# Batch 0's preparation in a fused cross-attention layer: all context loaded at once, key splits on VectorE, group 0's stack filled alone, twelve maxima inside quarter 0

## The chip, the cores and the metric

One core of a Trainium2 chip runs the whole program. The engines are TensorE (PE in the rows; PEld is its weight load), VectorE (DVE), ScalarE (ACT), GpSimd (POOL) and SyncE (SP), which in this kernel only issues DMAs. The metric is the device time of one execution in microseconds, lower is better.

## What is computed

Sixteen batches of a transformer layer with cross-attention: 512 queries and 1601 context rows of width 256, 16 heads of 16, and an MLP of width 1024, all in float32.

```python
B, Lq, _ = Q.shape
Lkv = KV.shape[1]
qn = _layer_norm(Q, ln_q_g, ln_q_b)
q = (qn @ Wq + bq).reshape(B, Lq, H, DH).transpose(0, 2, 1, 3)
k = (KV @ Wk + bk).reshape(B, Lkv, H, DH).transpose(0, 2, 1, 3)
v = (KV @ Wv + bv).reshape(B, Lkv, H, DH).transpose(0, 2, 1, 3)
scores = jnp.einsum('bhqd,bhkd->bhqk', q, k) / jnp.sqrt(jnp.float32(DH))
attn = jax.nn.softmax(scores, axis=-1)
ctx = jnp.einsum('bhqk,bhkd->bhqd', attn, v)
ctx = ctx.transpose(0, 2, 1, 3).reshape(B, Lq, D)
x = Q + (ctx @ Wo + bo)
h = _layer_norm(x, ln_ff_g, ln_ff_b)
ff = jax.nn.silu(h @ W1 + b1) @ W2 + b2
x = x + ff
```

## The kernel before

**Heads.** A batch has four quarters, one for each group of four heads (q = 0 to 3). Eight heads are a half (s = q // 2), with their own `k_stack[s]`, `q_stack[s]` and `v_sb[s]`. The context is handled in chunks c = 0 to 3 of 512, 512, 512 and 65 keys, and in 13 tiles of 128 keys; a quarter has 26 units, two for each tile.

**Scores in bf16.** Each key and query is split into three bf16 parts (`k_parts`, `q_parts`). ScalarE writes the float32 value to one of two buffers `whole` and the first part (L662, L663). GpSimd makes the other two with three subtractions (`read_parts`, L513 to L516) and counts them in `split`; ScalarE waits for the split before the last one, since `whole` has two buffers. SP then copies the parts by DMA into six 16-row slots of the stacks: `place` issues 12 DMAs for the first three slots of a group (L389), and `repeat`, which waits until all 24 of a group's `place` DMAs landed, issues six that copy the slots that repeat a part (L401).

**Maxima.** The softmax is shifted by the row's maximum. TensorE makes the scores once in the other orientation, 52 pieces m for a group (`make_rows`, L995, into two buffers `rows_ps`); VectorE reduces each (`read_rows`, L830). When 52 are in, VectorE negates them, TensorE turns them ("turn", L944), ScalarE copies them to `shift_parts`, and SP places them as three more rows of `q_stack` (`place_shift`, L424). The scores proper (L1010) wait for that. In steady state the maxima of the next group are made inside a quarter, 40 in units up to 19 and the first 12 (`EARLY`) of the group after it in the rest; `plan` spreads four over each tile.

**Side steps.** Everything else goes through the one PSUM bank `side`, in a fixed order of steps: TensorE fills it, ScalarE (for some steps VectorE) reads it, and TensorE waits (`side_read`) for the step before. Context transposes (`ctx`), keys (`k`), values (`v`), transposes of the normalised x (`x`) and queries (`q`) are steps.

**The opening of batch 0** is the `prologue` of each engine, and all is in program order on each. SP issues wk, context chunks 0 and 1, x, the other weights, seven columns of biases and gains (L366), two rows and eight small pieces; only then chunks 2 and 3, which reuse the buffers `ctx_nat` of the first two; then the stacks of both groups of half 0 (`fill_stacks`). TensorE makes the eight context steps, waits for all 22 loads (`loaded`), makes the product for the output bias (L1047), keys 0 to 3, x, the query and the four value steps; then 26 maxima of group 0, 26 more with the keys and the query of half 1 among them, the turn, and 12 maxima of group 1. VectorE sets the rows of ones in both stacks (L851), waits for all loads, and takes the moments of x. GpSimd normalises x and then splits the keys. Quarter 0 follows.

## Time and profile before

| | us |
|---|---|
| median of three runs | 3767.32 |
| lowest, highest | 3766.78, 3767.60 |
| profiled execution, its own time | 3763.43 |
| its span in the profile | 3761.6 |
| mean granted clock of TensorE | 0.989 |

The span is what the trace covers. In a row of the timeline, the first number is the start in us, the second the busy time, `x4` the number of instructions merged, and the bracket the idle time before them on that engine and what ended it. A float32 matmul shows as several records.

### The profile page before, as it was taken

The numbers are of one execution on the slowest core, as the hardware profiler recorded it, in microseconds if no ns is written. First come the engines' busy times: TensorE is split into PE (matmuls) and PEld (weight loads), VectorE is DVE, ScalarE is ACT, GpSimd is POOL, SyncE is SP. The second block draws the span as 40 slices with busy tenths as digits, with TensorE's granted clock in tenths as the row PEclk, the third lists the DMA queues.
The fourth block names the chain that finished last, engine by engine and source line by source line (L and its number), as shares of the span: only waits on it lengthen the run. The fifth ranks groups of instructions, "written<-read, shape, count | busy, mean of one in ns | idle before, by whom it ended". The sixth has DMA issues, their size and how long they took to land.

```text
span 3761.6 us, 52959 instructions
## 1 busy us (share of the span) xinstructions
PE 3559.0 (95%) x19880; PEld 1605.0 (43%) x19880; DVE 2483.2 (66%) x4568; ACT 2242.9 (60%) x2979; POOL 901.5 (24%) x1323
## 2 busy tenths in 40 slices
PE   3899999999999999999999999999999999999996
PEld 2233444444434444444444434444444444444434
DVE  2777767666676766667666676766667676676751
ACT  1366666656666565666656666566656656666562
POOL 2122313212231222313122231212313112231101
PEclk8899999999999999999999999999999999999999
DMA  3222212222122321212222122322212232121200
GB/s 84 45 50 40 46 32 61 41 47 45 32 51 39 65 41 32 47 33 58 41 58 38 30 50 37 64 41 36 49 32 54 42 64 39 27 48 34 41 7 12
DMA packets 121409, 162.99 MB, mean 43 GB/s; under 512 B 36912, under 2 KB 102464, under 8 KB 118080
## 3 DMA queue, kind: packets, MB, share of 16 engines
q1 hardware_dynamic: 121152, 159.60, 21.7%
q8 instruction: 157, 2.57, 0.3%
q14 instruction: 100, 0.82, 0.1%
HBM read 46.43 MB, written 8.39 MB: 15 GB/s over the span
## 4 chain that ended last, share of the span: by engine, by line
PE 81%; DVE 11%; ACT 4%; issue 2%; SPq 1%; POOL 1%; DMA 0%; ACTq 0%; POOLq 0%; DVEq 0%
PE o_ps L1029 20%; PE rows_ps L995 19%; PE scores L1010 14%; DVE chunk_max L830 8%; PE side L972 6%; PE side L969 6%; PE side L958 5%; PE side L950 4%; PE side L962 3%; ACT probs L717 2%; PE side L954 2%; DVE stats L748 1%; DVE resid L775 1%; PE side L941 1%; ACT ctxT L633 1%
## 5 line engine op out<-in xcount | busy, mean ns | idle before, releaser
L830 DVE TENSOR_REDUCE chunk_max<-rows_ps 128x1 f32<-128x512 f32 (+1 forms) x3328 | 2124.4, 666 | 1132.9 <-PE rows_ps L995 1124.4
L717 ACT ACTIVATE probs<-scores 128x1024 f32<-128x1024 f32 (+1 forms) x1664 | 1676.0, 1023 | 1174.5 <-PE scores L1010 1167.1
L995 PE MATMUL rows_ps<-k_stack,q_stack 96*128 96x512 bf16 (+1 forms) x4096 | 1220.1, 339 | 94.1 <-DVE chunk_max L830 50.6
L1010 PE MATMUL scores<-q_stack,k_stack 99*128 99x512 bf16 (+1 forms) x3328 | 1033.6, 379 | 3.3 <-ACT probs L717 2.7
L1029 PE MATMUL o_ps<-probs,v_sb 128*32 128x512 f32 x6656 | 886.5, 605 | 0.4 <-ACT probs L717 0.4
L995 PEld LDWEIGHTS rows_ps<-k_stack,q_stack 96*128 96x128 bf16 x4096 | 334.3, 97 | 1164.2 <-DVE chunk_max L830 930.7
L1010 PEld LDWEIGHTS scores<-q_stack,k_stack 99*128 99x128 bf16 (+1 forms) x3328 | 325.0, 100 | 300.4 <-issue 38.2
L513 POOL TENSOR_TENSOR rest<-whole,k_parts 128x512 f32<-128x512 f32 (+1 forms) x128 | 120.6, 942 | 1002.4 <-ACT k_parts L663 997.2
L565 POOL TENSOR_TENSOR attT<-o_sb,denom 128x512 f32<-128x512 f32 x64 | 81.2, 1268 | 945.3 <-DVE denom L817 945.3
L969 PE MATMUL side<-hT,w_sb 128*128 128x256 f32 x1024 | 272.6, 380 | 11.8 <-ACT tanh_sb L675 9.9
L972 PE MATMUL side<-w_sb,ffT 128*128 128x256 f32 x1024 | 259.2, 381 | 5.6 <-DVE ffT L793 5.0
L1029 PEld LDWEIGHTS o_ps<-probs,v_sb 128*32 128x32 f32 x6656 | 131.0, 108 | 296.8 <-issue 222.2
L958 PE MATMUL side<-wv_sb,ctxT 128*128 128x128 f32 (+1 forms) x1664 | 242.3, 278 | 4.6 <-ACT v_sb L649 2.0
L958 PEld LDWEIGHTS side<-wv_sb,ctxT 128*128 128x128 f32 (+1 forms) x1664 | 226.0, 187 | 46.7 <-ACT v_sb L649 11.4
L950 PE MATMUL side<-ctxT,wk_sb 128*128 128x512 f32 (+1 forms) x512 | 222.7, 519 | 9.2 <-ACT k_parts L663 9.2
L969 PEld LDWEIGHTS side<-hT,w_sb 128*128 128x128 f32 x1024 | 192.9, 190 | 63.2 <-ACT tanh_sb L675 17.0
L972 PEld LDWEIGHTS side<-w_sb,ffT 128*128 128x128 f32 x1024 | 191.5, 189 | 56.5 <-issue 7.7
L673 ACT ACTIVATE ffT<-side,half_b 128x256 f32<-128x256 f32 x256 | 121.5, 475 | 111.5 <-PE side L969 108.8
L528 POOL TENSOR_TENSOR newton<-rstd 128x2 f32<-128x2 f32 (+1 forms) x144 | 28.1, 195 | 591.6 <-DVE half_var L763 584.0
L962 PE MATMUL side<-wo_pad,attT 128*128 128x256 f32 x512 | 139.7, 389 | 5.0 <-POOL attT L565 3.9
L675 ACT ACTIVATE tanh_sb<-side,half_b 128x256 f32<-128x256 f32 x256 | 121.7, 475 | 0.0
L514 POOL TENSOR_TENSOR k_parts<-whole,k_parts 128x512 bf16<-128x512 f32 (+1 forms) x128 | 121.1, 946 | 0.1
(68 smaller groups left out, 1971.3 us busy)
## 6 DMA issues: line engine op xcount, KB each, us to landing
k_stack<-k_parts SPq DMA_DIRECT2D x768, 50.0 KB, 2.2
k_stack<-k_stack SPq DMA_DIRECT2D x192, 200.1 KB, 5.6
ctx_nat<-in_ctx SPq DMA_DIRECT2D x48, 512.0 KB, 4.0
q_stack<-q_parts SPq DMA_DIRECT2D x768, 16.0 KB, 1.8
q_stack<-q_stack SPq DMA_DIRECT2D x192, 64.0 KB, 3.4
x_nat<-in_x SPq DMA_DIRECT2D x16, 512.0 KB, 6.1
resid<-in_x SPq DMA_DIRECT2D x32, 256.0 KB, 2.8
out<-resid SPq DMA_DIRECT2D x32, 256.0 KB, 2.5
```

The costliest lines, as they stand in the source:

```text
L673: nc.scalar.activation(ffT[:, m, :], side[:, cols], ACT.Identity, bias=half_b1[:, m:m + 1], scale=0.5)
L675: last = nc.scalar.activation(tanh_sb[:, cols], side[:, cols], ACT.Tanh, bias=half_b1[:, m:m + 1], scale=0.5)
L717: nc.scalar.activation(probs[0:rows, (q + t) % 2, 2 * LQ * pair:2 * LQ * (pair + 1)], scores[0:rows, 2 * LQ * pair:2 * LQ * (pair + 1)], A ...
L830: nc.vector.tensor_reduce(dst, src, AX.X, ALU.max).then_inc(rows_read, 1)
L950: ins = nc.tensor.matmul(side[:, 0:width(arg)], wk_sb[:, j, P * s:P * (s + 1)], ctxT[:, j, CHUNK * arg:CHUNK * arg + width(arg)], start=(j ...
L958: ins = nc.tensor.matmul(side[0:rows, P * t:P * (t + 1)], ctxT[:, j, P * i:P * i + rows], wv_sb[:, j, P * s:P * (s + 1)], start=(j == 0), ...
L962: ins = nc.tensor.matmul(side[:, D * i:D * (i + 1)], attT[:, j, q0:q0 + P], wo_pad[:, j, :], start=(j == 0), stop=(j == 3))
L969: ins = nc.tensor.matmul(side[:, QH * i:QH * (i + 1)], w1_sb[:, j, P * m:P * (m + 1)], hT[:, j, :], start=(j == 0), stop=(j == KC - 1))
L972: ins = nc.tensor.matmul(side[:, D * i:D * (i + 1)], ffT[:, j, P * i:P * (i + 1)], w2_sb[:, j, :], start=(j == 0), stop=(j == FM - 1))
L995: last = nc.tensor.matmul(rows_ps[:, m % 2, d0:d0 + w], q_stack[s][0:STACK, h, P * t:P * (t + 1)], k_stack[s][0:STACK, h, k0:k0 + w], star ...
L1010: ins = nc.tensor.matmul(scores[0:keys_in(t), LQ * j:LQ * (j + 1)], k_stack[s][:, h, P * t:P * t + keys_in(t)], q_stack[s][:, h, :], start ...
L1029: last = nc.tensor.matmul(o_ps[32 * j:32 * j + 32, :], v_sb[q // 2][0:rows, t, col:col + 32], probs[0:rows, (q + t) % 2, LQ * j:LQ * (j + 1)],
```

## The change

- SP issues context chunk 0 first, then wk, chunk 1, x, chunks 2 and 3, wq and four columns; `loaded_first` counts wk, wq and the four columns (6). wv, the rows, the small pieces, w1, w2 and three columns follow and are counted in `loaded` (16). Chunks 2 and 3 go into a part of `ffT`, unused at that time, with semaphores of their own (`ctx_beside`).
- The steps follow a list `PROLOGUE`: context, k0, k1, v0, k2, v1, k3, v2, x0, x1, q0, v3, then half 1's keys and query among the maxima. TensorE and ScalarE wait for `loaded_first` before k0; TensorE waits for `loaded` before v0.
- VectorE takes the moments of x first, sets one stack's rows, splits half 0's four key chunks (`split_keys`), sets the other stack's rows. GpSimd keeps the query's split and half 1's.
- SP places group 0's keys, then repeats group 0; ScalarE issues group 0's 12 `place` DMAs of queries after the query's split. Group 1 follows on SP. `place` takes the queue as an argument and is defined once for both engines.
- The 12 maxima of group 1 move from the prologue into the first six tiles of quarter 0, six in a tile there instead of four.
- The product for the output bias moves behind the values, ahead of the maxima.

Lines of context are left out; declarations of the new semaphores and the removed local copy of `place` too.

```diff
@@ -57,7 +57,8 @@
-N_LOADS = 5 + 7 + 2 + 8
+N_FIRST = 2 + 4
+N_LOADS = 3 + 3 + 2 + 8
@@ -102,7 +103,13 @@
-BEFORE = sum(len(PREPARE[q]) for q in (1, 2, 3)) + 1
+PROLOGUE = ([(0, "ctx", (c, kc)) for c in range(NCH) for kc in range(KC)] + [(0, "k", 0), (0, "k", 1)]
+            + [(0, "v", 0), (0, "k", 2), (0, "v", 1), (0, "k", 3), (0, "v", 2), (0, "x", 0), (0, "x", 1), (0, "q", 0), (0, "v", 3)]
+            + [(1, "k", c) for c in range(NCH)] + [(1, "q", 0)])
+BESIDE_MAXIMA = NCH + 1
+BEFORE = len(PROLOGUE) + 1
@@ -157,6 +164,10 @@
+AHEAD = 2
@@ -170,11 +181,12 @@
-def plan(steps):
-    units, slot = [], 0
+def plan(steps, opening=False):
+    units, slot = [], -EARLY if opening else 0
+        per_tile = PER_TILE + AHEAD * (opening and t < EARLY // AHEAD)
@@ -185,7 +197,7 @@
-            while placed < PER_TILE and done * PER_TILE >= (placed + MAX_PHASE) * sum(costs):
+            while placed < per_tile and done * per_tile >= (placed + MAX_PHASE) * sum(costs):
@@ -357,16 +372,32 @@
+        def place(queue, dst, src, rows, g):
+            for part in range(PARTS):
+                slot = rows.index(part)
+                for h in range(4 * (g % 2), 4 * (g % 2) + 4):
+                    queue.dma_start(dst[16 * slot:16 * slot + 16, h, :], src[16 * h:16 * h + 16, part, :])\
+                        .then_inc(placed[g], 16)
-            def column(dst, src, n):
+            def column(dst, src, n, landed):
-                    sp.dma_start(dst[:, 0:n], src.rearrange("(c p) -> p c", p=P)).then_inc(loaded, 16)
+                    sp.dma_start(dst[:, 0:n], src.rearrange("(c p) -> p c", p=P)).then_inc(landed, 16)
-                if c < NCH - 1:
+                if b == 0 and c >= 2:
+                    dst = ffT[:, 4 * (c - 2):4 * (c - 2) + 4, :]
+                    if c < NCH - 1:
+                        sp.dma_start(dst, ctx[b, CHUNK * c:CHUNK * (c + 1), :].rearrange("(t p) d -> p t d", p=P))\
+                            .then_inc(ctx_beside[c - 2], 16)
+                    else:
+                        sp.dma_start(dst[0:LAST, 0, :], ctx[b, CHUNK * c:LK, :]).then_inc(ctx_beside[c - 2], 16)
+                elif c < NCH - 1:
@@ -406,13 +429,13 @@
-                place(k_stack[s], k_parts, K_ROWS, 2 * s)
+                place(sp, k_stack[s], k_parts, K_ROWS, 2 * s)
-                place(q_stack[s], q_parts, Q_ROWS, 2 * s)
-                place(k_stack[s], k_parts, K_ROWS, 2 * s + 1)
+                place(sp, q_stack[s], q_parts, Q_ROWS, 2 * s)
+                place(sp, k_stack[s], k_parts, K_ROWS, 2 * s + 1)
-                place(q_stack[s], q_parts, Q_ROWS, 2 * s + 1)
+                place(sp, q_stack[s], q_parts, Q_ROWS, 2 * s + 1)
@@ -432,15 +455,16 @@
-                sp.dma_start(wk_sb[:, :, :], wk.rearrange("(c p) n -> p c n", p=P)).then_inc(loaded, 16)
+                sp.dma_start(wk_sb[:, :, :], wk.rearrange("(c p) n -> p c n", p=P)).then_inc(loaded_first, 16)
-                for dst, src in ((wq_sb, wq), (wv_sb, wv), (w1_sb, w1), (w2_sb, w2)):
-                    sp.dma_start(dst[:, :, :], src.rearrange("(c p) n -> p c n", p=P)).then_inc(loaded, 16)
-                for dst, src, n in ((bq_c, bq, KC), (bk_c, bk, KC), (b1_c, b1, FM), (gq_c, gq, KC), (cq_c, cq, KC),
-                                    (gf_c, gf, KC), (cf_c, cf, KC)):
-                    column(dst, src, n)
+                load_ctx(0, 2)
+                load_ctx(0, 3)
+                sp.dma_start(wq_sb[:, :, :], wq.rearrange("(c p) n -> p c n", p=P)).then_inc(loaded_first, 16)
+                for dst, src, n in ((bk_c, bk, KC), (bq_c, bq, KC), (gq_c, gq, KC), (cq_c, cq, KC)):
+                    column(dst, src, n, loaded_first)
+                sp.dma_start(wv_sb[:, :, :], wv.rearrange("(c p) n -> p c n", p=P)).then_inc(loaded, 16)
@@ -451,11 +475,18 @@
-                for c in (2, 3):
-                    sp.wait_ge(side_ready, index(PREPARE[1], "ctx", (c - 2, KC - 1)) + 1)
-                    load_ctx(0, c)
-                fill_stacks(0, 0)
+                for dst, src in ((w1_sb, w1), (w2_sb, w2)):
+                    sp.dma_start(dst[:, :, :], src.rearrange("(c p) n -> p c n", p=P)).then_inc(loaded, 16)
+                for dst, src, n in ((b1_c, b1, FM), (gf_c, gf, KC), (cf_c, cf, KC)):
+                    column(dst, src, n, loaded)
+                sp.wait_ge(split, NCH)
+                place(sp, k_stack[0], k_parts, K_ROWS, 0)
+                repeat(0, 0)
+                place(sp, k_stack[0], k_parts, K_ROWS, 1)
+                place(sp, q_stack[0], q_parts, Q_ROWS, 1)
+                repeat(0, 1)
@@ -578,17 +609,15 @@
-                for s in range(2):
-                    pool.memset(v_sb[s][:, :, :], 1.0).then_inc(ones_set, 1)
+                pool.memset(v_sb[0][:, :, :], 1.0).then_inc(ones_set, 1)
+                normalise_x(0)
+                pool.memset(v_sb[1][:, :, :], 1.0).then_inc(ones_set, 1)
+                for n, (s, kind, arg) in enumerate(PROLOGUE):
+                    if (s, kind) == (0, "q") or s == 1:
+                        read_parts(0, s, (0, 0), n, arg if kind == "k" else NCH)
-                normalise_x(0)
-                n = 0
-                for q, (_, s) in ((1, PREPARED[1]), (2, PREPARED[2]), (3, PREPARED[3])):
-                    splits(0, s, (0, n), PREPARE[q])
-                    n += len(PREPARE[q])
@@ -684,18 +713,25 @@
-                n = 0
-                for q in (1, 2, 3):
-                    for k, (_, _, kind, arg) in enumerate(PREPARE[q]):
-                        if (q, kind, arg) == (1, "k", 0):
-                            act.wait_ge(loaded, 16 * N_LOADS)
-                            nc.scalar.mul(bq_c[:, :], bq_c[:, :], 1.0 / DH ** 0.5).then_inc(setup_done, 1)
-                            nc.scalar.mul(half_b1[:, :], b1_c[:, :], 0.5).then_inc(setup_done, 1)
-                            act.wait_ge(setup_done, 3)
-                            act.wait_ge(ones_set, 4)
-                        side_step(0, PREPARED[q][1], (0, n), k, kind, arg)
-                    n += len(PREPARE[q])
+                for n, (s, kind, arg) in enumerate(PROLOGUE):
+                    if (s, kind, arg) == (0, "k", 0):
+                        act.wait_ge(loaded_first, 16 * N_FIRST)
+                        nc.scalar.mul(bq_c[:, :], bq_c[:, :], 1.0 / DH ** 0.5).then_inc(setup_done, 1)
+                        act.wait_ge(setup_done, 1)
+                    if (s, kind, arg) == (0, "v", 0):
+                        act.wait_ge(ones_set, 1)
+                    if (s, kind, arg) == (1, "k", 0):
+                        act.wait_ge(loaded, 16 * N_LOADS)
+                        nc.scalar.mul(half_b1[:, :], b1_c[:, :], 0.5).then_inc(setup_done, 1)
+                        act.wait_ge(setup_done, 2)
+                    side_step(0, s, (0, 0), n, kind, arg)
+                    if (s, kind) == (0, "q"):
+                        act.wait_ge(split, NCH + 1)
+                        place(act, q_stack[0], q_parts, Q_ROWS, 0)
+                n = len(PROLOGUE)
@@ -801,6 +837,19 @@
+            def split_keys(c):
+                w, off = width(c), CHUNK * c
+                src, parts = whole[:, c % 2, 0:w], [k_parts[:, part, off:off + w] for part in range(PARTS)]
+                dve.wait_ge(side_read, PROLOGUE.index((0, "k", c)) + 1)
+                wait(dve, split, c)
+                seq.inc(nc.vector.tensor_tensor(rest[:, 0:w], src, parts[0], ALU.subtract))
+                seq.inc(nc.vector.tensor_tensor(parts[1], src, parts[0], ALU.subtract))
+                dve.wait_ge(dve_seq, seq.value)
+                nc.vector.tensor_tensor(parts[2], rest[:, 0:w], parts[1], ALU.subtract).then_inc(split, 1)
@@ -844,32 +893,33 @@
+                for stage in range(STAGES):
+                    x_moments(0, stage)
+                for s in range(2):
+                    nc.vector.memset(k_stack[s][STACK:ROWS, :, :], 1.0).then_inc(stack_ones, 1)
+                    if s == 0:
+                        for c in range(NCH):
+                            split_keys(c)
-                nc.vector.memset(ones, 1.0).then_inc(setup_done, 1)
-                for s in range(2):
-                    nc.vector.memset(k_stack[s][STACK:ROWS, :, :], 1.0).then_inc(ones_set, 1)
+                nc.vector.memset(ones, 1.0).then_inc(bv_spread, 1)
-                dve.wait_ge(setup_done, 3)
+                dve.wait_ge(bv_spread, 1)
-                for stage in range(STAGES):
-                    x_moments(0, stage)
-                for m in range(EARLY):
-                    read_rows(0, 1, m)
-                for u, work in enumerate(plan(steps)):
+                for u, work in enumerate(plan(steps, b == q == 0)):
@@ -919,7 +969,10 @@
-                        pe.wait_ge(ctx_landed[arg[0] % 2], b * 32 + 16 * (arg[0] // 2 + 1))
+                        if b == 0 and arg[0] >= 2:
+                            pe.wait_ge(ctx_beside[arg[0] - 2], 16)
+                        else:
+                            pe.wait_ge(ctx_landed[arg[0] % 2], 16 if b == 0 else b * 32 - 16 + 16 * (arg[0] // 2 + 1))
@@ -938,7 +991,8 @@
-                    ins = nc.tensor.transpose(side[:, P * t:P * t + rows], ctx_nat[0:rows, c % 2, t, P * j:P * (j + 1)],
+                    place_of = ffT[:, 4 * (c - 2):4 * (c - 2) + 4, :] if b == 0 and c >= 2 else ctx_nat[:, c % 2, :, :]
+                    ins = nc.tensor.transpose(side[:, P * t:P * t + rows], place_of[0:rows, t, P * j:P * (j + 1)],
@@ -1034,36 +1088,39 @@
-                n, m = 0, 0
-                for q in (1, 2, 3):
-                    for k, (_, _, kind, arg) in enumerate(PREPARE[q]):
-                        if (q, kind, arg) == (1, "k", 0):
-                            pe.wait_ge(ones_set, 4)
-                            pe.wait_ge(loaded, 16 * N_LOADS)
-                            pe.wait_ge(bv_spread, 4)
-                            for g in range(4):
-                                last = nc.tensor.matmul(o_ps[:, 0:D], probs[:, 0, P * g:P * (g + 1)], wo_pad[:, g, :],
-                                                        start=(g == 0), stop=(g == 3))
-                            last.then_inc(bo_product, 1)
-                        if q == 3:
-                            while m < FIRST_MAXIMA + 5 * k:
-                                make_rows(0, 0, m)
-                                m += 1
-                        side_step(0, PREPARED[q][1], (0, n), k, kind, arg)
-                    n += len(PREPARE[q])
+                m, beside = 0, len(PROLOGUE) - BESIDE_MAXIMA
+                for n, (s, kind, arg) in enumerate(PROLOGUE):
+                    if (s, kind, arg) == (0, "k", 0):
+                        pe.wait_ge(loaded_first, 16 * N_FIRST)
+                    if (s, kind, arg) == (0, "v", 0):
+                        pe.wait_ge(loaded, 16 * N_LOADS)
+                    if n == beside:
+                        pe.wait_ge(bv_spread, 5)
+                        for g in range(4):
+                            last = nc.tensor.matmul(o_ps[:, 0:D], probs[:, 0, P * g:P * (g + 1)], wo_pad[:, g, :],
+                                                    start=(g == 0), stop=(g == 3))
+                        last.then_inc(bo_product, 1)
+                    if n >= beside:
+                        while m < FIRST_MAXIMA + 5 * (n - beside):
+                            make_rows(0, 0, m)
+                            m += 1
+                    side_step(0, s, (0, 0), n, kind, arg)
-                for m in range(EARLY):
-                    make_rows(0, 1, m)
+                pe.wait_ge(stack_ones, 2)
+                pe.wait_ge(ones_set, 2)
-                for u, work in enumerate(plan(steps)):
+                for u, work in enumerate(plan(steps, b == q == 0)):
```

On VectorE, at the start of the program, before: ones, both stacks' rows of ones, `bv` spread, the output bias, moments of x.

```order
L848 MEMSET denom 128x128
L851 MEMSET k_stack 3x12808 x2
L856 TENSOR_SCALAR probs<-denom,bv_pad 128x128 x4
L860 TENSOR_TENSOR bo_row<-o_ps,bo_row 128x256
L748 BN_STATS stats<-x_nat 128x6 x4
L756 BN_AGGR moments<-stats 128x2 x4
```

On VectorE, at the start of the program, now:

```order
L784 BN_STATS stats<-x_nat 128x6 x4
L792 BN_AGGR moments<-stats 128x2 x4
L795 TENSOR_SCALAR half_var<-moments 128x4
L797 TENSOR_SCALAR rstd<-half_var 128x4
L799 TENSOR_SCALAR half_var<-half_var 128x4
L900 MEMSET k_stack 3x12808
L848 TENSOR_TENSOR rest<-whole,k_parts 128x512
L849 TENSOR_TENSOR k_parts<-whole,k_parts 128x512
L851 TENSOR_TENSOR k_parts<-rest,k_parts 128x512
```

The moments moved ahead of everything, one stack's ones stand between them and the splits, and three subtractions for each chunk are new there; the other stack's ones come behind the last split.

On SP, behind the loads, the filling of half 0's stacks before (groups 0 and 1: keys, queries, repeats) and the shift of group 0:

```order
L389 DMA k_stack<-k_parts 16x1601 x12
L389 DMA q_stack<-q_parts 16x512 x12
L389 DMA k_stack<-k_parts 16x1601 x12
L401 DMA k_stack<-k_stack 16x6404 x3
L401 DMA q_stack<-q_stack 16x2048 x3
L389 DMA q_stack<-q_parts 16x512 x12
L401 DMA k_stack<-k_stack 16x6404 x3
L401 DMA q_stack<-q_stack 16x2048 x3
L424 DMA q_stack<-shift_parts 1x4x512 x3
```

On SP, the same place now:

```order
L380 DMA k_stack<-k_parts 16x1601 x12
L424 DMA k_stack<-k_stack 16x6404 x3
L424 DMA q_stack<-q_stack 16x2048 x3
L380 DMA k_stack<-k_parts 16x1601 x12
L380 DMA q_stack<-q_parts 16x512 x12
L424 DMA k_stack<-k_stack 16x6404 x3
L424 DMA q_stack<-q_stack 16x2048 x3
L447 DMA q_stack<-shift_parts 1x4x512 x3
```

Group 0's repeats stand behind its 12 key DMAs alone; its 12 query DMAs left this queue for ScalarE's, and all of group 1 comes after.

On TensorE, from the last maxima of group 0 into quarter 0, before:

```order
L944 MATMUL side<-ident_bf,neg_parts 12x128 x4
L995 MATMUL rows_ps<-k_stack,q_stack 128x512 x12
L1010 MATMUL scores<-q_stack,k_stack 128x512 x2
L995 MATMUL rows_ps<-k_stack,q_stack 128x65 x4
L958 MATMUL side<-wv_sb,ctxT 128x128 x4
```

On TensorE, the same place now:

```order
L998 MATMUL side<-ident_bf,neg_parts 12x128 x4
L1064 MATMUL scores<-q_stack,k_stack 128x512 x2
L1049 MATMUL rows_ps<-k_stack,q_stack 128x512
L1012 MATMUL side<-wv_sb,ctxT 128x128 x2
L1049 MATMUL rows_ps<-k_stack,q_stack 128x512
L1012 MATMUL side<-wv_sb,ctxT 128x128 x2
```

The maxima between the turn and the first scores are gone from there, and one stands between every two products of the values.

## Rows read from the trace of the kernel before

**Rows 1.** The page, its chain that ended last, by engine:
```profile
PE 81%; DVE 11%; ACT 4%; issue 2%; SPq 1%; POOL 1%; DMA 0%; ACTq 0%; POOLq 0%; DVEq 0%
```
**Rows 2.** The chain in order of time, 0 to 150 us: start, us, what:
```profile
42.92 4.84 POOL x_nat L533 x4
...
89.10 2.69 DMA q_stack<-q_stack
...
91.92 0.60 PE rows_ps L995
...
109.62 3.57 PE side L950 x4
...
136.97 0.58 PE side L944 x4
```
**Rows 3.** Busy time by windows (PE, PEld, DVE, ACT, POOL; granted clock, DMA share, GB/s):
```profile
92.00:113.00 21.00, 18.21 (x37) 4.07 (x37) 16.16 (x26) 0.00 (x0) 0.00 (x0) 0.50 0.31 47
```
**Rows 4.** The timeline, 0 to 31 us: context steps and SP's issues:
```profile
5.74 1.09 PE L941 MATMUL side<-ident,ctx_nat 128*128 128x128 f32 x4 [5.74 <-DMA ctx_nat<-in_ctx]
...
9.30 1.12 PE L941 MATMUL side<-ident,ctx_nat 128*128 128x128 f32 x4 [0.68 <-ACT ctxT L633]
...
12.04 3.60 SPq L366 DMA_DIRECT2D gq_c<-in_L_xattn_ln_q_g  x1
...
22.16 0.43 SPq L371 DMA_DIRECT2D ctx_nat<-in_ctx  x1
...
30.73 0.37 PE L941 MATMUL side<-ident,ctx_nat 65*128 65x65 f32 x1 [0.30 <-ACT ctxT L633]
```
**Rows 5.** DMA issues, 0 to 35 and 59 to 92 us: KB each, us to landing:
```profile
x_nat<-in_x SPq DMA_DIRECT2D x1, 512.0 KB, 7.6
...
q_stack<-q_parts SPq DMA_DIRECT2D x16, 16.0 KB, 1.8
```
**Rows 6.** The timeline, 44 to 67 us: steps of keys, x, query, values:
```profile
44.19 1.98 PE L950 MATMUL side<-ctxT,wk_sb 128*128 128x512 f32 x4 [1.35 <-ACT k_parts L663]
...
57.40 1.12 PE L948 MATMUL side<-ident,x_nat 128*128 128x128 f32 x4 [0.87 <-ACT qnT L637]
...
59.38 3.63 PE L954 MATMUL side<-qnT,wq_sb 128*128 128x512 f32 x4 [0.87 <-ACT qnT L637]
...
67.09 2.05 PE L958 MATMUL side<-wv_sb,ctxT 128*128 128x128 f32 x16 [0.68 <-ACT v_sb L649]
```
**Rows 7.** The timeline of SP's queue, 59 to 92 us:
```profile
67.92 7.84 SPq L389 DMA_DIRECT2D q_stack<-q_parts  x12
...
83.39 2.52 SPq L401 DMA_DIRECT2D k_stack<-k_stack  x3
```
**Rows 8.** VectorE: its timeline, 0 to 40 us, and a group by line:
```profile
3.70 10.73 DVE L851 MEMSET k_stack<- 3x12808 bf16 x1 [2.72 <-issue]
17.05 10.73 DVE L851 MEMSET k_stack<- 3x12808 bf16 x1 [2.62 <-issue]
...
36.82 1.39 DVE L748 BATCH_NORM_STATS2 stats<-x_nat 128x6 f32<-128x256 f32 x4
...
39.07 0.17 DVE L763 TENSOR_SCALAR half_var<-half_var 128x4 f32<-128x4 f32 x1
...
L793 DVE SCALAR_TENSOR_TENSOR ffT<-tanh_sb,ffT 128x512 f32<-128x512 f32 x128 | 87.5, 683 | 47.4 <-ACT tanh_sb L675 47.4
```
**Rows 9.** The timeline, 137 to 146 us: the shift's issues, the first scores:
```profile
138.19 1.90 SPq L424 DMA_DIRECT2D q_stack<-shift_parts  x3
...
145.46 1.06 PE L1010 MATMUL scores<-q_stack,k_stack 99*128 99x512 bf16 x2
```
**Rows 10.** The timeline of quarter 0, 161 to 166 us:
```profile
161.94 0.61 PE L995 MATMUL rows_ps<-k_stack,q_stack 96*128 96x512 bf16 x2
...
163.11 0.39 PE L995 MATMUL rows_ps<-k_stack,q_stack 96*128 96x512 bf16 x1 [0.35 <-DVE chunk_max L830]
...
165.73 2.52 DVE L830 TENSOR_REDUCE chunk_max<-rows_ps 128x1 f32<-128x512 f32 x4 [0.84 <-PE rows_ps L995]
```

9 lines of the change are left out of this document (3 added, 6 removed).

## The prediction, made before the changed kernel was run

> **What bounds the kernel now.** I read the page first: the profiled execution has a span of 3761.6 us (the table), and TensorE (PE) carries most of the chain that ended last [rows 1]. So a change outside the steady quarters can only shorten the opening. I then read the chain of waits for the first 150 us. It shows three things to look for. GpSimd's four normalisations stand on it (42.92 us), then DMA issues up to 89.10 us, and only at 91.92 us does TensorE compute the first row of scores for the maxima [rows 2]. The 21 us behind run at a granted clock of 0.50, the 1.2 GHz level, with TensorE and VectorE taking turns [rows 3]. Everything before 91.92 us is latency on a chain of single steps. That chain is what the change rebuilds; nothing in it touches batches 1 to 15.
>
> The sum goes by stages: the first row (91.92 us before), the stretch from there to the turn (45.05 us, from 91.92 to 136.97), the turn up to the first scores, and quarter 0.
>
> **Loading and transposing.** Before, chunks 2 and 3 of the context were issued behind 21 other loads, at 22.16 us [rows 4], and TensorE stood still for them. Now all four chunks are near the head of SP's queue. The first chunk's transposes began at 5.74 us [rows 4]; it is now issued half a microsecond earlier and ahead of wk's 256 KB, for which I take 4.9 us (bounds 4.4 and 5.7). In a row of the timeline, the busy time and the idle time before it together are the repeat time of a step: 1.12 + 0.68 = 1.80 us for four transposes and their copy, 0.37 + 0.30 = 0.67 for 65 columns [rows 4]. Six and two of them: 10.8 + 1.3, so the keys can begin at 17.0 us. They need six early loads, two weights and four columns of biases and gains. Before, the column loads were held in SP's queue (gq's issue took 3.60 us [rows 4]) behind 4.25 MB; now 2.6 MB stand ahead of them. x took 7.6 us to land with 1.3 MB ahead of it [rows 5], so 2.6 MB should be in by 12 us. I take no wait; the bound is 1.2 us, for a landing at 18.2, a little behind the end of gq's issue before, 15.6.
>
> **Keys, values and queries, now interleaved on the one bank `side`.** TensorE and ScalarE alternate, so each step costs its repeat time. A step of keys: 1.98 + 1.35, 3.34 us with rounding. The same four matmuls take 1.99 us at 2.4 GHz and 3.63 us at 1.2 GHz (the query step), so the first, after transposes at the low level, costs 4.98. A step of values: 2.05 + 0.68 = 2.73 us. The two x steps: 1.12 + 0.87 = 1.99 us each at the low level [rows 6]. The 65-column key step lies between 0.67 and 3.34; I take 1.2, because its matmuls are an eighth as long. On the path: k0 4.98, k1 3.34, v0 2.73, k2 3.34, v1 2.73, k3 1.2, v2 2.73 = 21.05, which brings 38.0 us; x0 and x1 (3.98) make it 42.0. From the first query matmul to SP's first issue of query parts it was 59.38 to 67.92 = 8.54 us [rows 6, 7] (matmuls, two activations, GpSimd's three subtractions; the query's split stays on GpSimd, and there is nothing ahead of it there). That gives 50.6 us at the low level throughout; with the high level kept after the keys it is 2.6 us less (1.0 on x, 1.65 on q). Context transposes with a gap of 0.7 us never left the low level, keys with gaps of 1.4 us kept the high one. I take the middle, 49.2 us.
>
> What hides beside this path? First, VectorE's split of the keys, taken from GpSimd. Moments of x start when x lands, at 9.9 us, and take 2.4 (36.82 to 39.24 [rows 8]); then comes the memset of k_stack's last three rows. The profile gives that memset as 10.73 us, but the two of them start at 3.70 and 17.05, 13.35 us apart, and the gap of 2.62 us between is put down to nothing [rows 8]. I take 13.35, so VectorE is free at 25.7 us and splits chunk 0 by 27.8 (three operations of 0.68 us, the nearest row being the product of two SBUF operands [rows 8]). ScalarE needs that split before it writes k2's result, at 30.0 us. Slack 2.2 us. The other splits keep up, the last ends about 36.2 us, and SP issues group 0's keys from then to 43.8, before the queries are ready. By the Trainium skill (VectorE: DVE Perf Modes, Zero memsets can be issued as uint32) a memset takes one cycle per element whatever the type, 12808 of them at 0.96 GHz, an estimate of 13.3 us; this trace agrees by the distance of the starts, not by the row's own length. By the row alone VectorE would be free at 23.1 and the slack 4.8, with the same total.
>
> Second, TensorE's wait before v0 for all 16 remaining loads, at 25.3 us. Behind it stand v0, k2 and all that follows. The 2 MB of w1 and w2, formerly early, are now issued after the small loads. Before, the queue was through with the same loads at 22.16 us [rows 4], and 4 us more let them land. With less stall in the columns, of which gq's alone held 3 us, I put it at 24, so no cost; bounds 0 and +6. Third, normalised x: moments at 12.3 plus 8.5 us on GpSimd (39.24 to 47.76 [rows 2, 8]), 20.8, needed at 38. Fourth, ScalarE's and TensorE's product for the output bias: VectorE's second memset now starts at 36.2 and ends at 49.6; its inputs follow in 1 us and TensorE's eight matmuls take 3.8, so 55, before the rows.
>
> **Filling group 0.** Before, SP issued q parts (7.84 us), then group 1's keys (twelve more), then the repeated slots. Now ScalarE issues the q parts at 49.2 and SP goes straight to the repeats, which wait for them. At SP's 0.65 us an issue that is 7.84 [rows 7]; the last is issued at 56.5 and lands 1.8 us later [rows 5]: 58.3. From SP's first repeat to TensorE's first row it was 83.39 to 91.92 = 8.53 us [rows 2, 7]. First row: **66.8 us, 25.1 earlier**. No issue by ScalarE is in this trace. Its price is bounded by the cheapest and the dearest issue of SP: 0.43 and 3.60 us [rows 4]; I take 0.65, the same transfers. The Trainium skill (DMA: Bandwidth & Descriptors, Issuing engines are not separate DMA queues) says that a second issuing engine saves only the sequencer's time. Here SP is idle from 43.8 us, so by that this part saves nothing; what saves 7.8 us is that group 1's keys no longer stand ahead of the repeats.
>
> Behind the repeats SP issues group 1's parts (from 64.6, 7.84 each: keys to 72, queries to 80, landed by 82). ScalarE's first key of the second half overwrites them and waits for that; it comes at 66.8 + 17.7 + 3.6 = 88.1 (before, 91.92 to 109.62, and 3.57 of matmuls [rows 2]). Slack 6 us, and nothing else in it changed. So the 45.05 us stretch should be the same.
>
> **Turn and quarter 0.** Before, 12 maxima of group 1 ran from 137.55 to the first scores at 145.46 [rows 9] and hid the shift's way. Now scores follow the turn directly and wait for it: the three issues began at 138.19 and took 1.90, and the last of them, begun at 139.5, needs 1.8 to land and 0.1 to wake TensorE: 141.4 in the old time [rows 5, 9]. Gain 4.1 us. The 12 maxima go into tiles 0 to 5 of quarter 0, two more in each. In tiles 0 to 2, TensorE is busy throughout with values: one matmul of a row takes 0.39, two 0.61 [rows 10], so one more costs 0.22 and a tile 0.45. Tiles 3 to 5 repeat every 3.36 us or little more, with four reads of 2.52 us and 0.84 idle on VectorE [rows 10]; six reads take 3.78 and some 0.4 idle remains: +0.9 a tile. Sum 4.0, plus 0.4 for a start at 1.2 GHz after an idle TensorE: **+4.4**. Bounds: 12 x 0.22 = 2.6, and 12 x 3.36 / 4 = 10.1, where each costs a quarter of a tile.
>
> **Sum.** -25.1 - 4.1 + 4.4 = -24.8 us. The profiled execution took 3763.43 us (span 3761.6), the median of the three runs is 3767.32; by the span I expect 3736.8, by the median **3742.5**.
>
> **Rivals.**
> 1. *The loads set v0.* If the last of the 16 lands at 31 us, the path is 5.7 us later: 3748. For it: a column's issue took 3.60 us, and b1's 1024 small elements are now among the last. Against it: less data ahead. In the range.
> 2. *The maxima cost nothing in quarter 0 and issues are cheap.* Lower bounds, -1.8 for quarter 0, -2.6 for ScalarE's issues (0.43 each), -1.3 for the clock: 3737.
> 3. *The gain is given back behind the first row.* If group 1's filling is 20 us later than I put it, the first key of the second half waits 14 us and the total is about 3757; with 24 us it is 3761, no change. Nothing in the rows is that slow.
> 4. *Slower.* One mechanism: ScalarE's queue pays for each of its twelve issues what gq's column cost, 3.60 us. Then q is in place 35.4 us later, and the total is 3742.5 + 35.4 = 3778. It decides from 0.65 + 24.8 / 12 = 2.7 us an issue. Against it: that price was paid with 4 MB queued, and here the rings are empty.
> 5. *The change does not do what it says,* as VectorE's splits or v0 wait for something unseen for over 17 us: near 3760.
>
> **How the numbers follow.** Forecast 0.70, rival 1 0.13, rival 2 0.09, rivals 3 and 5 0.05, rival 4 0.03. The range takes in the forecast's bounds and rivals 1 and 2: 3733 to 3753. A difference within 0.2%, 7.5 us, is about what a measurement of this kernel can't tell from none. Faster 0.93, same 0.04, slower 0.03.
>
> **What would show it.** In the changed kernel's trace: context transposes from 5 to 17 us without a pause; v0's matmuls at about 25 us; SP's first key parts at 36, ScalarE's issues at 49, the first row at 67; the first scores about 50 us after it, some 4 us behind the turn; quarter 0 some 4.4 us longer; from there on the same rows 24.8 us earlier. What would make me wrong: an issue on ScalarE that costs far from 0.65 us, v0 held by the loads, or tiles 0 to 5 that grow by over 1 us each.

## The result, and the profile after

The changed kernel takes 3745.86 us (median of 4 runs, 3743.92 to 3747.18), the kernel before, run beside it, 3767.46 (4 runs, 3766.78 to 3768.86). The ratio is 0.9942 [0.9925, 0.9959]: 21.6 us faster. The forecast was 3742.5, with 3733 to 3753 as its range.

The profiled execution of after took 3746.01 us, with a span of 3744.2, 17.4 less than before. Its page, the chain that ended last by engine; GpSimd and SP's queue, with 1% each before [rows 1], stand at 0%:

```profile
PE 82%; DVE 11%; ACT 4%; issue 2%; DMA 0%; POOL 0%; SPq 0%; ACTq 0%; DVEq 0%
```

The chain in order of time, 0 to 120 us (start, us, what), answers to [rows 2]:

```profile
0.72 4.06 DMA ctx_nat<-in_ctx
4.92 1.10 PE side L995 x4
...
17.09 3.77 PE side L1004 x4
...
22.26 3.79 PE side L1004 x4
...
37.59 2.06 PE side L1012 x16
...
43.37 3.69 PE side L1008 x4
...
58.98 1.83 DMA q_stack<-q_parts
...
66.45 2.64 DMA q_stack<-q_stack
...
117.16 1.78 DMA q_stack<-shift_parts
119.07 1.01 PE scores L1064 x2
```

The four normalisations on GpSimd that stood at 42.92 us are gone from it. From 4.92 us on the path is the one bank `side`, TensorE and ScalarE in turn, as the forecast had it. The queue rows on SP and ScalarE (timeline, 38 to 118 us) answer to [rows 7, 9]:

```profile
38.22 8.21 SPq L380 DMA_DIRECT2D k_stack<-k_parts  x12
...
51.96 7.63 ACTq L380 DMA_DIRECT2D q_stack<-q_parts  x12
...
60.83 2.40 SPq L424 DMA_DIRECT2D k_stack<-k_stack  x3
...
69.23 1.01 PE L1049 MATMUL rows_ps<-k_stack,q_stack 96*128 96x512 bf16 x2 [12.51 <-DMA q_stack<-q_stack]
...
115.45 2.30 SPq L447 DMA_DIRECT2D q_stack<-shift_parts  x3
...
119.07 1.01 PE L1064 MATMUL scores<-q_stack,k_stack 99*128 99x512 bf16 x2 [4.26 <-DMA q_stack<-shift_parts]
```

Laid beside the same marks of before, in us from the span's start:

| mark | before | after | difference |
|---|---|---|---|
| chunk 2's first transposes | 26.50 | 12.06 | -14.4 |
| first key matmuls | 36.23 | 17.09 | -19.1 |
| query matmuls | 59.38 | 43.37 | -16.0 |
| first issue of the queries' parts | 67.92 | 51.96 | -16.0 |
| SP's repeats begin | 83.39 | 60.83 | -22.6 |
| first row | 91.92 | 69.23 | -22.7 |
| turn | 136.97 | 114.23 | -22.7 |
| first scores | 145.46 | 119.07 | -26.4 |
| shift at the end of quarter 0 | 188.57 | 168.31 | -20.3 |
| shift of the last quarter but one | 3642.70 | 3623.26 | -19.4 |
| end of the span | 3761.6 | 3744.2 | -17.4 |

So the opening and quarter 0 gave 20.3 us. The other 2.9 us of this pair lie where the change touches nothing: about 0.9 in the steady quarters, mostly one wait of TensorE for a context load (0.51 us before, at 1523; 1.53 us after, at 1504), and 2.0 in the last 119 us. There the granted clock differs, as the windows of the last 10 us show (busy time of PE, PEld, DVE, ACT, POOL; clock; DMA share; GB/s), before and then after:

```profile
3751.60:3761.60 10.00, 6.65 (x31) 5.51 (x29) 0.69 (x1) 0.00 (x0) 0.00 (x0) 1.00 0.08 26
```
```profile
3734.20:3744.20 10.00, 6.61 (x25) 5.26 (x23) 0.69 (x1) 0.00 (x0) 0.00 (x0) 0.84 0.08 26
```

Over the profiles below, this end (shift of the last quarter but one to the end of the span) took 118.9 to 124.4 us. It adds to any comparison of single executions, so the experiments are read by their marks before it.

### The profile page after: what moved, and what is told of

Same layout as the page of the kernel before. It is cut to its first block, busy times and chain, and to the rows that moved or that the text cites. A ratio compares the mean times of both kernels' runs of the same rounds, so it can differ in the third digit from the quotient of the medians.

```text
span 3744.2 us, 52962 instructions
## 1 busy us (share of the span) xinstructions
PE 3560.6 (95%) x19880; PEld 1608.2 (43%) x19880; DVE 2488.8 (66%) x4580; ACT 2243.0 (60%) x2979; POOL 890.5 (24%) x1311
## 4 chain that ended last, share of the span: by engine, by line
PE 82%; DVE 11%; ACT 4%; issue 2%; DMA 0%; POOL 0%; SPq 0%; ACTq 0%; DVEq 0%
PE o_ps L1083 20%; PE rows_ps L1049 19%; PE scores L1064 14%; DVE chunk_max L879 8%; PE side L1026 6%; PE side L1023 6%; PE side L1012 5%; PE side L1004 5%; PE side L1016 3%; ACT probs L753 2%; PE side L1008 2%; DVE stats L784 1%; DVE resid L811 1%; PE side L995 1%; ACT ctxT L662 1%
## 5 line engine op out<-in xcount | busy, mean ns | idle before, releaser
L544 POOL TENSOR_TENSOR rest<-whole,k_parts 128x512 f32<-128x512 f32 x124 | 116.8, 942 | 995.0 <-ACT k_parts L692 990.5
L829 DVE SCALAR_TENSOR_TENSOR ffT<-tanh_sb,ffT 128x512 f32<-128x512 f32 x128 | 87.5, 683 | 47.4 <-ACT tanh_sb L704 47.4
```

## The experiments

Nine kernels make one edit each, all on the changed kernel but one; two try a faster order; one is the changed kernel again. What is read from each, in us ("to turn" runs from the first row to the turn, "scores to shift" from the first scores to SP's issue of the shift at the end of quarter 0, and "shift at" is the time of that issue):

| kernel | first row | to turn | turn to scores | scores to shift | shift at |
|---|---|---|---|---|---|
| before | 91.92 | 45.05 | 8.49 | 43.11 | 188.57 |
| changed | 69.23 | 45.00 | 4.84 | 49.24 | 168.31 |
| changed again (e12) | 68.73 | 45.16 | 4.76 | 49.04 | 167.69 |
| e1 maxima back | 69.50 | 45.16 | 8.49 | 44.61 | 167.76 |
| e2 splits on GpSimd | 67.19 | 45.16 | 4.84 | 49.00 | 166.19 |
| e3 queries by SP | 67.13 | 45.16 | 4.36 | 47.63 | 164.28 |
| e4 context late | 80.18 | 45.14 | 4.76 | 49.00 | 179.08 |
| e5 group 1's keys first | 67.61 | 44.72 | 4.84 | 48.89 | 166.06 |
| e6 busy turn | 67.12 | 43.54 | 4.83 | 46.97 | 162.46 |
| e7 busy opening | 69.12 | 44.86 | 4.77 | 47.75 | 166.50 |
| e8 busy before rows | 67.29 | 44.93 | 4.76 | 49.14 | 166.12 |
| e9 maxima alone, on before | 90.73 | 43.52 | 4.26 | 48.90 | 187.41 |
| e10 queries first | 60.13 | 46.63 | 4.36 | 49.20 | 160.32 |
| e11 both | 59.87 | 45.15 | 4.76 | 47.38 | 157.16 |

**How far an opening repeats itself.** The changed kernel, e12, e1 and e6 have the same instructions up to the first row, which came at 69.23, 68.73, 69.50 and 67.12. The difference stands in one row of the timeline, the second chunk's key matmuls. First the changed kernel's:

```profile
22.26 3.78 PE L1004 MATMUL side<-ctxT,wk_sb 128*128 128x512 f32 x4 [1.42 <-ACT k_parts L692]
```

and e6's:

```profile
22.26 1.98 PE L1004 MATMUL side<-ctxT,wk_sb 128*128 128x512 f32 x4 [1.42 <-ACT k_parts L692]
```

They start in the same hundredth, with the same matmuls and waits before them, and took 3.78 us at the 1.2 GHz level and 1.98 at 2.4. The changed kernel, e12 and e1 drew the first, e2 to e6 and e8 the second. What sets it isn't visible in the rows. e12's own pair of readings doesn't decide between chance and its rival, since both executions of the changed kernel drew the low level; that e6, and up to this step e3, e5 and e8 too, drew the high one with the same instructions speaks for chance. Openings are therefore compared with others that drew the same: 67.1 to 67.6, or 68.7 to 69.5.

Of each edit only the telling lines are shown. ` ...` marks lines left out; the definitions of the extra matmuls and, in e1, the matching lines of VectorE are left out too.

**e4: chunks 2 and 3 of the context loaded behind the other loads, as before.**

```
-                load_ctx(0, 2)
-                load_ctx(0, 3)
 ...                                     (wq, wv, the columns, wo, bv)
+                load_ctx(0, 2)
+                load_ctx(0, 3)
```

> The changed kernel with context chunks 2 and 3 issued last of all loads (at some 19.3 us, behind the column whose issue took 3.78 us). My theory: the chain from loads to queries is what sets the first row, so it moves by what the transposes of chunk 2 move: from 12.06 to 23.5 us, 11.5 us later, less 1 to 2 us because TensorE may be quicker after it; the first row at 80. Rival: another chain (VectorE's memset and splits, SP's key parts) is as long, and the first row moves by less than 6 us.

Its timeline, 10 to 26 us:

```profile
10.25 1.12 PE L995 MATMUL side<-ident,ctx_nat 128*128 128x128 f32 x4 [0.68 <-ACT ctxT L662]
25.29 1.09 PE L995 MATMUL side<-ident,ffT 128*128 128x128 f32 x4 [13.93 <-DMA ffT<-in_ctx]
```

TensorE stands 13.93 us for the load. Chunk 2 begins 13.2 us later than in the changed kernel (12.06), and the first row comes at 80.18, 13.1 behind e6's like-clocked 67.12: the delay passes through whole. Of the first row's 22.7 us, the context's early load carries 13.

**e5: group 1's keys placed before the repeats again.**

```
-                repeat(0, 0)
                 place(sp, k_stack[0], k_parts, K_ROWS, 1)
+                repeat(0, 0)
```

> The changed kernel with group 1's key parts on SP ahead of group 0's repeats, as before the change. In the changed kernel SP idles from 46.4 us until the queries have landed at 60.8. My theory: the 7.5 us of issues fit into that idle time, and the first row stays at 69.2 us; what the prediction gave to filling group 0 alone was really won by the queue being empty that early. Rival, the prediction's words: group 1's keys ahead of the repeats cost 7.5 us, first row at 76.7.

The two queues, 36 to 62 us:

```profile
36.47 16.02 SPq L380 DMA_DIRECT2D k_stack<-k_parts  x24
...
50.31 7.64 ACTq L380 DMA_DIRECT2D q_stack<-q_parts  x12
...
59.19 2.40 SPq L424 DMA_DIRECT2D k_stack<-k_stack  x3
```

All 24 issues fit between the keys' readiness at 36.5 and 52.5, while the queries are still being issued; the repeats wait for those at 59.19. The first row is at 67.61, 0.4 to 0.5 behind the others. The query matmuls alone took 3.78 here and 3.36 in e6, which covers that. As long as the queries are issued by another engine, filling group 0 alone is worth nothing.

**e3: group 0's queries issued by SP**, between group 0's keys and the repeats, and group 1 behind them.

```
+                sp.wait_ge(split, NCH + 1)
+                place(sp, q_stack[0], q_parts, Q_ROWS, 0)
 ...
-                        act.wait_ge(split, NCH + 1)
-                        place(act, q_stack[0], q_parts, Q_ROWS, 0)
```

> The changed kernel with group 0's twelve query placements issued by SP, behind its key parts, instead of by ScalarE. SP is idle from 46.4 to 60.8 us there. My theory: the same first row, 69.2 us within 0.3, since the issues begin at 52.0 either way. Rival: ScalarE's queue is what lets them start early; then the first row is 1 us or more later.

```profile
36.56 8.50 SPq L380 DMA_DIRECT2D k_stack<-k_parts  x12
...
50.01 7.46 SPq L380 DMA_DIRECT2D q_stack<-q_parts  x12
...
58.71 2.40 SPq L424 DMA_DIRECT2D k_stack<-k_stack  x3
```

First row 67.13, the same. SP is idle from 45.1 to 50.0, so it is no help that ScalarE takes these twelve issues. e3 and e5 each remove one of two measures and lose nothing. Before, the twelve issues of group 1's keys stood between the queries and the repeats, where they cost the 6.6 us by which that way shortened (67.92 to 83.39, now 51.96 to 60.83). Either measure moves them from there. With both undone they would stand on the path again; that was not tried.

**e2: key splits back on GpSimd.**

```
-                    if (s, kind) == (0, "q") or s == 1:
+                    if kind in ("k", "q"):
 ...
-                    if s == 0:
-                        for c in range(NCH):
-                            split_keys(c)
```

> The changed kernel with half 0's key splits back on GpSimd (3.5 us a chunk instead of 2.1). My theory: with values between the keys the splits have slack on either engine. GpSimd is free at 21.5 us, splits chunk 0 from 22.3 to 25.8, chunk 1 by 30.9, chunk 2 by 37.1, the last by 38.8; ScalarE's k2 at 32.27 and k3 at 37.01 find theirs done. SP's first key parts go out 0.8 us later (39.0), the first row stays at 69.2, and so does all behind it. Rival: the splits on VectorE were what the interleaved steps needed; then k2 or k3 wait for GpSimd and the first row comes 2 to 5 us later.

First row 67.19, the same. GpSimd, which normalises x from 15.24 and clears v_sb behind it, is ready for chunk 0 when its copy comes:

```profile
20.02 1.74 POOL L614 MEMSET v_sb<- 128x1963 f32 x1
22.28 1.16 POOL L544 TENSOR_TENSOR rest<-whole,k_parts 128x512 f32<-128x512 f32 x1 [0.52 <-ACT k_parts L692]
```

VectorE, behind its memset, did this split at 24.84. It is faster at each operation (0.69 us for 1.16) and starts later; with values between the keys, neither is waited for.

**e7: TensorE kept busy in the opening**, by five small matmuls of the identity, their result unused, behind each context step but the last chunk's and behind v2, x0 and x1.

```
+                    if kind == "ctx" and arg[0] < NCH - 1:
+                        busy_ident(5)
+                    if (kind, arg) == ("v", 2) or kind == "x":
+                        busy_ident(5)
```

> The changed kernel with five extra small matmuls (128 columns, bf16, result unused) in the gap behind each context step of 512 columns, behind v2 and behind each x step. My theory: k0 (3.75 us), k1 (3.78) and q0 (3.68) ran at 1.2 GHz because TensorE idles in the gaps between; filled, k0 and k1 take 2.0 each and q0 2.0, and the first row comes 5 us earlier, at 64. Rival: the granted clock does not follow these gaps; then the three steps keep 3.7 us and the first row is where it was or 0.5 us later.

Its timeline, 15 to 46 us:

```profile
15.53 1.96 PE L1004 MATMUL side<-ctxT,wk_sb 128*128 128x512 f32 x4 [0.40 <-ACT ctxT L662]
18.91 1.98 PE L1004 MATMUL side<-ctxT,wk_sb 128*128 128x512 f32 x4 [1.42 <-ACT k_parts L692]
24.18 3.78 PE L1012 MATMUL side<-wv_sb,ctxT 128*128 128x128 f32 x16 [3.29 <-DMA cf_c<-in_L_xattn_ln_ff_b]
28.70 3.78 PE L1004 MATMUL side<-ctxT,wk_sb 128*128 128x512 f32 x4 [0.73 <-ACT v_sb L678]
```

The clock rises, and the keys begin 1.6 us earlier and run at 2.4 GHz. Then v0 waits 3.29 us for the last of the 16 loads, and v0, k2 and most of v1 run at the low level. The gain is more than used up: the first row comes at 69.12, where 64 was expected and e6 has 67.12. This is the first rival's wait, on a faster path: the loads are in at 24.1 us, 3.4 before the changed kernel needs them and 1.6 before e6 does, whose v0 starts at 25.69.

**e8: TensorE kept busy before the first row**, by ten float32 matmuls behind the output bias's product, 54.75 to 63.5 us.

```
+                        busy_keys(10)
```

> The changed kernel with ten extra float32 matmuls of 512 columns (result unused) on TensorE between the output bias product and the first row, where it idles 12.5 us. They take about 1.8 us each at 1.2 GHz and 1.0 at 2.4, so some 12 us. The first 26 rows then start at 2.4 GHz; at that level a row repeats every 0.60 us instead of 0.70. My theory: the clock falls back after some rows, since TensorE is busy 0.39 of 0.60 us there, so the stretch from the first row to the turn is 0.5 to 1.5 us shorter than 45.0. Rival: it stays at 2.4 GHz through all 26 rows and the k step behind them: 2.5 + 1.9 = 4.4 us shorter. Other rival: VectorE's reads alone set the pace, no change.

```profile
67.29 0.59 PE L1062 MATMUL rows_ps<-k_stack,q_stack 96*128 96x512 bf16 x2 [3.75 <-DMA q_stack<-q_stack]
68.45 1.20 PE L1062 MATMUL rows_ps<-k_stack,q_stack 96*128 96x512 bf16 x2 [0.57 <-DVE chunk_max L879]
```

The first pair takes 0.59 us instead of 1.01 and the next are at the low level again. The stretch stays 44.93, where 0.5 to 1.5 us less was expected; TensorE and VectorE take turns on the rows there as in [rows 3]. The windows of the first rows, the changed kernel's and e8's (clock 0.50 and 0.53):

```profile
69.30:87.00 17.70, 14.92 (x33) 3.03 (x33) 15.75 (x26) 0.00 (x0) 0.00 (x0) 0.50 0.40 62
...
67.30:85.00 17.70, 14.72 (x33) 3.23 (x34) 15.91 (x26) 0.00 (x0) 0.00 (x0) 0.53 0.40 62
```

A start at the high level doesn't lift this stretch.

**e1 and e9: the twelve maxima.** e1 puts them back behind the turn in the changed kernel; e9 makes that part of the change alone in the kernel before.

```
+                for m in range(EARLY):
+                    make_rows(0, 1, m)
-                for u, work in enumerate(plan(steps, b == q == 0)):
+                for u, work in enumerate(plan(steps)):
```

> The changed kernel with group 1's 12 maxima put back between the turn and the first scores, and four maxima a tile in quarter 0. In the changed kernel the way from the turn's first matmul to the first scores is 4.84 us and tile 0 takes 7.15. My theory: moving the maxima won 3.65 us there (8.49 before) and lost 6.13 in quarter 0, so by itself it is a loss of 2.5 us. Here the first scores come 3.7 us later than in the changed kernel (122.7), tile 0 takes 4.8, and the shift's issue at the end of quarter 0 is at 165.8 instead of 168.31. The prediction's own terms (4.1 won, 4.4 lost) give 168.0. Rival: the slow tile 0 comes from the shorter opening as a whole and not from the idle TensorE ahead of it; then tile 0 stays at some 6.5 us and the issue comes at 170.

> The kernel before with one part of the change alone: group 1's 12 maxima moved from behind the turn into tiles 0 to 5 of quarter 0. From the experiment that put them back in the changed kernel I now expect: 3.65 us less between turn and scores (4.8 instead of 8.49), tiles 2 to 5 longer by 3.2 us as in every run with six maxima a tile, and 0.9 to 2.9 us more up to the first product with the values, by TensorE's clock there. The shift's issue at the end of quarter 0, 50.4 us behind the first one before, comes 0.5 to 2.5 us later. By the prediction's terms it would be 0.3 later; by my theory after the first trace, 2.5.

In e1 the way from the turn to the scores is 3.65 us longer and quarter 0 is 4.63 shorter: it comes out 1.0 ahead of the changed kernel, 0.7 ahead of e12. In e9, against before, 4.23 are gained at the turn and 5.79 lost in quarter 0: 1.6 behind. That looks like a loss of about 1 us by the move, but single executions don't settle it: from the turn to the shift at the end of quarter 0, the ten kernels with the maxima moved and nothing added behind the turn took 51.99 (e3) to 54.08 us (changed), and the two with them in the old place 51.60 (before) and 53.10 (e1).

Part of it is the same everywhere. From the first to the fifth product with values the tiles take 4.63, 2.62, 3.36 and 3.59 us in the kernel before, and 5.05, 3.14, 4.29 and 4.92 in every kernel with the maxima moved, 3.2 more. VectorE's rows of the changed kernel, 139 to 144 us, show why:

```profile
139.84 3.66 DVE L879 TENSOR_REDUCE chunk_max<-rows_ps 128x1 f32<-128x512 f32 x6 [0.63 <-PE rows_ps L1049]
```

Six maxima fill a tile that took 3.36 before with four of them and 0.84 us idle [rows 10]. The rest is tile 0. From the first scores to the first product it takes 8.23 us before, 9.74 in e1 and 11.15 in the changed kernel; two things act here, the two further maxima and the clock. The first 7 us of scores in before, e1 and e3:

```profile
145.46:152.46 7.00, 7.00 (x42) 5.31 (x41) 4.26 (x8) 3.66 (x4) 0.00 (x0) 0.81 0.30 59
123.15:130.15 7.00, 7.00 (x32) 5.03 (x31) 3.27 (x6) 2.74 (x4) 0.00 (x0) 0.59 0.32 61
116.65:123.65 7.00, 6.88 (x34) 4.89 (x35) 4.35 (x7) 3.31 (x4) 0.00 (x0) 0.78 0.41 72
```

At like clocks the two maxima cost some 1.1 us: e1 (0.59) takes 9.74, e5 and e9 (0.60) 10.81 and 10.82; before (0.81) takes 8.23, e11 (0.83) and e3 (0.78) 9.31 and 9.55. The move as a whole then costs 0.1 to 0.7 us (3.2 + 1.1, less the 3.65 to 4.23 won at the turn), less than what the clock alone changes here.

**e6: TensorE kept busy behind the turn**, by ten matmuls on the stacks, their result unused. They fill most of the idle time before the scores.

```
+                busy_rows(10)
```

> The changed kernel with ten extra matmuls (96 rows, 512 columns, bf16, their result unused) on TensorE behind the turn, where it idles 4.3 us for the shift. My theory: tile 0 takes 7.15 us because TensorE comes out of idleness at 1.2 GHz; kept busy it is at 2.4 GHz at the first scores or within a microsecond, tile 0 takes 5.2 to 5.6 and the shift's issue at the end of quarter 0 comes 1.5 to 2 us earlier than 168.31. Rival: tile 0 is long because six maxima in it wait for VectorE; then nothing changes, or it gets later by what the extra matmuls overrun.

Its timeline, and then its window of the first 7 us of scores:

```profile
110.66 0.58 PE L998 MATMUL side<-ident_bf,neg_parts 128*12 128x128 bf16 x4 [3.01 <-DVE neg_parts L893]
111.18 4.45 PE L1038 MATMUL scores<-k_stack,q_stack 96*128 96x512 bf16 x10
115.49 1.01 PE L1077 MATMUL scores<-q_stack,k_stack 99*128 99x512 bf16 x2
```
```profile
115.50:122.50 7.00, 6.88 (x40) 4.88 (x40) 5.03 (x8) 3.66 (x4) 0.00 (x0) 0.88 0.43 78
```

The changed kernel's windows, the idle way and the same 7 us:

```profile
114.00:119.00 5.00, 0.59 (x4) 0.33 (x4) 0.08 (x1) 0.57 (x1) 0.00 (x0) 0.50 0.02 4
119.00:126.00 7.00, 6.93 (x26) 4.91 (x27) 2.77 (x4) 2.21 (x3) 0.00 (x0) 0.54 0.39 69
```

With like busy time, 40 matmuls pass at a clock of 0.88 and 26 at 0.54. Tile 0's first product comes 8.89 us behind the scores, not 11.15, and the quarter is 2.3 us shorter (46.97). How much of that the extra matmuls brought is open. Of the ten kernels that idle there, eight had 0.54 to 0.60 as the clock of these 7 us, but e3 and e7, with the same code, 0.78 and 0.77, and quarters of 47.63 and 47.75: against those e6 gains 0.7 us. Nor is a busy TensorE enough: in e1 it is busy for 4.44 of the 5 us before the scores, and the clock behind them is 0.59. The two kernels with extra matmuls (e6, and e11 with 0.83) have the highest values, so that they help is likely.

**e10 and e11: a faster order.** e10 makes all keys first, then x and the query, and the values last, where the queries' DMAs hide them. SP issues the queries.

```
+PROLOGUE = ([...ctx...] + [(0, "k", c) for c in range(NCH)]
+            + [(0, "x", 0), (0, "x", 1), (0, "q", 0)] + [(0, "v", c) for c in range(NCH)]
```

> The changed kernel with the order of steps k0, k1, k2, k3, x0, x1, q0, v0 to v3, and the query placements issued by SP. v0, v1 and v2 stand on the way from the keys to the query in the changed kernel, 3 x 2.73 = 8.2 us. My theory: that way sets the first row, the splits on VectorE keep up without the values between (2.1 us against 3.34 a key step) and the second memset and the bias product (done by 52) stay hidden, so the first row comes at 59 (8.2 us before 67.2) and the whole is 3737 by median, against 3744 to 3746. Rival 1: the splits now hold k2 and k3, since VectorE is free only at 24.9; first row 62 to 64. Rival 2: the values, made behind the query, delay the bias product past 59, and the first row waits for that.

```profile
33.91 3.78 PE L1009 MATMUL side<-qnT,wq_sb 128*128 128x512 f32 x4 [0.87 <-ACT qnT L668]
...
42.59 7.90 SPq L380 DMA_DIRECT2D q_stack<-q_parts  x12
...
51.73 2.40 SPq L424 DMA_DIRECT2D k_stack<-k_stack  x3
...
60.13 1.01 PE L1050 MATMUL rows_ps<-k_stack,q_stack 96*128 96x512 bf16 x2 [8.90 <-DMA q_stack<-q_stack]
```

The first row is 7 us before the like-clocked 67.1 of e3. The expectation was 59, and 3737 for the whole. Whole: 3739.35 us (4 runs, 3738.57 to 3739.67), ratio to before 0.9923 [0.9909, 0.9936].

e11 adds extra matmuls in the context steps, at x0 and x1, and behind the turn.

> The same with extra matmuls whose result is unused in the gaps of the context steps and behind x0 and x1 (five small ones each), and ten behind the turn. In the earlier runs these made k0, k1 and q0 take 2.0 us instead of 3.7 and tile 0 about 1.7 us shorter; what they won in the opening was lost to the wait for the loads at v0, which now comes after the query. My theory: 1.5 (contexts) + 1.7 + 0 to 1.8 + 1.7 off the query's end, first row at 54 to 56, the whole 3731 to 3734. Rival: the first row is then set by VectorE's memset and the splits (first split not before 24.9, the last behind the third's by 3), and no more than 2 us are won.

Whole: 3735.19 us (5 runs, 3734.59 to 3739.14), ratio 0.9914 [0.9900, 0.9927], the best of all. The first row gained only 0.3 us (59.87, expected 54 to 56), for the reason its rival gave. VectorE's split begins when its memset ends, at 25.52, and the last chunk's keys wait for it:

```profile
25.52 0.69 DVE L849 TENSOR_TENSOR rest<-whole,k_parts 128x512 f32<-128x512 f32 x1
...
28.95 1.12 PE L1005 MATMUL side<-ctxT,wk_sb 128*128 128x65 f32 x4 [4.80 <-ACT k_parts L694]
```

1.8 of its 3.2 us at the end of quarter 0 come from scores to shift (47.38 for 49.20; e3 and e7 had 47.63 and 47.75 without extra matmuls). Another 1.5 are in the stretch (45.15 for 46.63), which also differs between kernels with the same code there, 43.5 to 46.6. The intervals of e10 and e11 overlap: that e11 is the faster is likely, not shown.

**e12: the changed kernel again**, measured beside e10 and e11.

> The changed kernel again, beside the two above. My theory: its first profile had k1 at 1.2 GHz (3.78 us instead of 1.98), which the other kernels' profiles with the same opening did not; so the first row is at 67.2 or 69.2 by chance, and the time lies between 3742 and 3747, 20 to 24 us below the kernel before. Rival: the first row is at 69.2 each time, and the others were quicker by what they changed.

3746.5 us (5 runs, 3745.04 to 3747.47), ratio 0.9941 [0.9929, 0.9954], against 3739.35 and 3735.19. Its runs lie clear above those of e10 and e11.

## Why the prediction was right, and where it was off

The sign and the size held: -24.8 us forecast, -21.6 measured, and -20.3 in the part of the trace that the change touches.

**Steps that held.** Context: transposes from 4.92 us (forecast 4.9) and keys from 17.09 (17.0), without a pause. The memset: x's moments start at 8.93 and the first split at 24.84, as these two rows around it show:

```profile
8.93 1.40 DVE L784 BATCH_NORM_STATS2 stats<-x_nat 128x6 f32<-128x256 f32 x4 [8.93 <-DMA x_nat<-in_x]
...
14.08 10.73 DVE L900 MEMSET k_stack<- 3x12808 bf16 x1 [2.72 <-issue]
```

The last operation on the moments ended at 11.36, so 13.5 us lie between, not the row's 10.73: the distance of the starts was the right reading. The loads: in at 24.1 by e7 (24). ScalarE's issues: 7.63 / 12 = 0.64 us each (0.65); the fourth rival, 3.60 each, falls. From the repeats to the first row 8.40 (8.53), the stretch 45.00 (45.05).

**Terms mis-sized.** First, the clock in the opening. The forecast had the second key step at 3.34 us, on the rule that gaps of 1.4 us keep the high level. In the changed kernel it took 3.78 + 1.42 = 5.2, 1.9 more, though in e2 to e6, e8 and e10, with the same gap, it took 1.98. So that gaps of 1.4 us keep the high level holds in some executions only. Another 0.3 us came before it and 0.5 with the query, which took 3.68 us where the middle between the levels had been put down; 0.3 were won behind the issues. That makes the 2.4 us by which the first row was late (69.23 for 66.8). The forecast allowed 1.3 us either way for the clock on x and the query, and nothing for a key step. In the executions that kept the high level the first row came at 67.1 to 67.6, 0.3 to 0.8 from the forecast.

Second, turn to scores: 4.84 for 4.43, as the three issues took 2.30 for 1.90. Third, quarter 0: +6.1 for +4.4. The later tiles were nearly right: the four steps behind the first product grew by 0.42, 0.52, 0.93 and 1.33 us and the fifth not at all, 3.2 together, where 3.55 was put down for tiles 1 to 5. Tile 0 was wrong: its first product comes 2.9 us later behind the scores, and 0.45 for two maxima and 0.4 for a start at 1.2 GHz were put down. At like clocks the two maxima cost 1.1. The other 1.8 go with the clock, 0.81 in before's first 7 us and 0.54 in the changed kernel's; by e3 it could as well have been 0.2. Both kernels start their scores at the low level (1.06 and 1.01 us for two), and what differs is how soon they leave it.

These add up: 2.4 + 0.4 + 1.7 = 4.5, the difference of -20.3 from -24.8. Most of it is how the clock fell in this execution: e3, the same code but for the queue of twelve issues, drew the high level at both places and has its shift at 164.28, 24.3 us before the kernel before.

**A reason that was wrong, under a right total.** The sentence that 7.8 us are saved because group 1's keys no longer stand ahead of the repeats holds only in part. The way did get 6.6 us shorter, but e5 puts the keys ahead of the repeats again at no loss. What counts is that they don't come between the queries' issues and the repeats. There the rule quoted from the Trainium skill (DMA: Bandwidth & Descriptors, Issuing engines are not separate DMA queues) held: ScalarE's issuing saved nothing (e3). So did the split on VectorE (e2). And the order with values between keys and query, costed as given, was the dearest thing left in the opening: 7 us (e10).

The marks give the first row's 22.7 us in four parts. The early context: 14.4. From there to the keys: 4.7, since this product for the output bias stood between them before and now lies beside the queries' issues:

```profile
32.69 3.75 PE L1047 MATMUL o_ps<-wo_pad,probs 128*128 128x256 f32 x8 [1.58 <-DVE probs L856]
```
```profile
52.94 3.78 PE L1103 MATMUL o_ps<-wo_pad,probs 128*128 128x256 f32 x8 [3.88 <-DVE probs L910]
```

(the first is of before, the second the same product in the changed kernel). From the keys to the query: 3.1 lost, 1.9 of it by the low clock of the second key step (e6 loses 1.3). Before, TensorE waited 6.39 us there for a copy that waited for GpSimd's splits, behind its normalisations; that is gone, but three steps of values, 8.2 us, came in. And group 1's issues: 6.6.

By e2, the splits needn't have moved for that wait to go. x's moments no longer wait for the second memset, GpSimd has normalised x by 20.1, and that was enough.

## What to carry to other kernels

On a path of single dependent steps, a load that is issued earlier pays in full (13.2 us earlier, 13.1 gained), and reassigning work that nobody waits for pays nothing (e2, e3); look for what stands between two steps of the path in the same queue or on the same bank, here the values. Compare one-time parts by marks, and against executions whose clock fell alike: with the same instructions, the first row alone differed by 2.4 us, and the 7 us behind the first scores ran at 0.54 to 0.78. A difference of 1 or 2 us between two single executions of such a part is not yet an effect of the edit.

## What the runs showed of the hardware

The same four matmuls, after the same rows, took 1.98 us in one execution and 3.78 in another. The same holds at the end of the program, where identical code took 118.9 to 124.4 us. Small matmuls in the gaps were enough to raise the clock in the opening (e7: four transposes in 0.66 us, not 1.12), but ten matmuls ahead of the alternating rows were not enough to keep it there (e8). A memset of 3x12808 bf16 keeps VectorE for 13.4 us, although its row says 10.73 and the 2.7 before it are put down to "issue". The issue of a column gain behind w1 and w2 cost 3.78 us in SP's queue (3.60 before), while its neighbours cost 0.58 and 0.84; the four columns issued ahead of these 2 MB cost 0.50 to 0.70. Behind the turn, the granted clock of the first 7 us of scores was 0.54 to 0.60 or 0.77 to 0.78 with an idle TensorE ahead of them, 0.59 and 0.81 with the twelve maxima there, 0.83 and 0.88 with ten extra matmuls.
